# A small language-model tower in float32: block orders in the expert part and the latent stage, a small Silu at a turn's end, and identity products in TensorE's waits

## The reference, cut to what matters

```python
h = _L0_tok_ref(x, ...)                      # embedding, positions, layer norm
h = h + _L0_attn_ref(_layernorm(h), ...)     # attention, 12 heads, fake-quantised
h = h + _L0_ffn_ref(_layernorm(h), ...)      # feed-forward of layer 0: 3 causal attention experts, gated
h = h + _L1_attn_ref(_layernorm(h), ...)     # latent stage: linear attention, then silu(xn @ w1) * (xn @ w2) @ w3
h = h + _L1_ffn_ref(_layernorm(h), ...)      # attention, router, 8 experts

# in _L0_ffn_ref, with x normalised
qk = x @ Wqk + bqk ; ve = x @ Wv[e] + bv[e] ; gate = softmax(relu(x @ Wg1 + bg1) @ Wg2 + bg2)
# in _L1_attn_ref, 192 -> 512 -> 192
latent = silu(x_norm @ w_comp)
ffn_out = silu(xn @ w1) * (xn @ w2) @ w3
# in _L1_ffn_ref, each token in its two best experts, 192 -> 768 -> 192
h = gelu(xm @ w1[e] + b1[e], approximate=False)
out = out + combine[:, e:e + 1] * (h @ w2[e] + b2[e])
```

## Time and profile before

| what | value |
|---|---|
| median of three runs | 2048.46 us |
| the profiled execution | 2050.18 us |
| its span, first to last instruction | 2048.5 us |
| TensorE (PE) busy | 1606.7 us, 78% |
| VectorE (DVE) busy | 1309.3 us, 64% |
| ScalarE (ACT) busy | 976.1 us, 48% |
| GpSimd (POOL) busy | 400.1 us, 20% |
| mean granted TensorE clock | 0.862 |

### The profile page before, as it was taken

The page is one execution under the profiler, slowest core; times in us unless marked ns, Lnnn a source line. Parts: engine busy times, 40 slices in busy tenths (PEclk is TensorE's granted clock), DMA queues, the critical chain, the costliest instruction groups (busy, mean ns, idle before and its releaser), DMA issues.

```text
span 2048.5 us, 36437 instructions
## 1 busy us (share of the span) xinstructions
PE 1606.7 (78%) x12540; PEld 1167.9 (57%) x12540; DVE 1309.3 (64%) x4361; ACT 976.1 (48%) x2773; POOL 400.1 (20%) x494
## 2 busy tenths in 40 slices
PE   0166673978888668888888868999999769999996
PEld 0032222865665445555555547777877647777774
DVE  7898885878888777887787844666666622222121
ACT  1275998944444444455555423344444324444441
POOL 7302332000000100000000010222222223333332
PEclk9985555557788779999999978999999979999998
DMA  3000001049960000000000000000000057777775
GB/s 73 16 1 1 1 1 17 6 95 185 181 97 0 1 1 1 0 0 0 0 0 0 0 26 1 25 24 23 23 23 27 20 138 178 179 181 175 185 175 128
DMA packets 136262, 113.00 MB, mean 55 GB/s; under 512 B 29416, under 2 KB 128456, under 8 KB 136136
## 3 DMA queue, kind: packets, MB, share of 16 engines
q1 hardware_dynamic: 119320, 91.70, 19.4%
q0 software_dynamic: 16864, 20.33, 5.2%
HBM read 69.19 MB, written 45.94 MB: 56 GB/s over the span
## 4 chain that ended last, share of the span: by engine, by line
PE 51%; DVE 27%; ACT 15%; issue 4%; POOL 1%; DMA 0%; DVEq 0%; ACTq 0%; POOLq 0%; SPq 0%
ACT bank L716 8%; PE bank L2331 8%; PE bank L1007 6%; PE bank L2316 5%; PE bank L2320 4%; PE bank L1987 3%; PE bank L1000 2%; PE bank L1217 2%; PE bank L1665 2%; PE bank L966 2%; DVE R L1839 2%; DVE WK L1581 1%; DVE R L1581 1%; PE bank L2015 1%; PE bank L2000 1%
## 5 line engine op out<-in xcount | busy, mean ns | idle before, releaser
L1047 POOL TENSOR_TENSOR WK<-WK,mhalf 128x2 f32<-128x2 f32 (+1 forms) x96 | 78.0, 813 | 837.4 <-DVE WK L1505 328.3
L2368 ACT ACTIVATE R<-bank,R 128x256 f32<-128x256 f32 x234 | 98.3, 472 | 217.9 <-PE bank L2320 217.9
L2220 DVE SCALAR_TENSOR_TENSOR WK<-bank,R,WK 128x192 f32<-128x192 f32 x78 | 28.9, 412 | 266.6 <-PE bank L2331 266.6
L716 ACT ACTIVATE bank<-bank,nbias,sc 128x128 f32<-128x128 f32 x384 | 168.9, 952 | 21.7 <-POOL nbias L528 21.7
L1007 PE MATMUL bank<-WK,R 96*128 96x256 f32 x576 | 159.1, 421 | 17.0 <-ACT WK L973 11.0
L2249 POOL DMA_INDIRECT moe_sum<-WK x78 | 121.6, 1558 | 258.4 <-DVE WK L2220 197.2
L2331 PE MATMUL bank<-R 128*128 128x192 f32 x936 | 169.1, 331 | 0.0
L716 ACT ACTIVATION_READ_ACCUMULATOR bank<-bank,nbias,sc 128x1 f32 x384 | 162.2, 727 | 0.0
L2331 PEld LDWEIGHTS bank<-R 128*128 128x128 f32 x936 | 150.1, 190 | 13.3 <-issue 13.3
L1007 PEld LDWEIGHTS bank<-WK,R 96*128 96x128 f32 x576 | 111.3, 204 | 41.6 <-ACT WK L973 15.6
L2316 PE MATMUL bank<-R 128*128 128x256 f32 x468 | 126.1, 392 | 1.1 <-ACT R L2359 1.1
(11 more groups left out here) (496 smaller groups left out, 3971.2 us busy)
## 6 DMA issues: line engine op xcount, KB each, us to landing
moe_rows_in<-zeros SPq DMA_DIRECT2D x1, 25026.0 KB, 146.2
R<-in_L_ffn_w SPq DMA_DIRECT2D x39, 576.0 KB, 5.0
R<-in_L_ffn_w SPq DMA_DIRECT2D x39, 384.0 KB, 3.0
R<-moe_rows_in SPq DMA_DIRECT2D x39, 194.0 KB, 4.7
R<-in_L_ffn_w SPq DMA_DIRECT2D x78, 96.0 KB, 3.7
R<-in_L_ffn_b SPq DMA_DIRECT2D x39, 96.0 KB, 5.4
moe_sum<-resid POOLq DMA_DIRECT2D x16, 192.0 KB
moe_sum<-WK POOLq DMA_INDIRECT x78, 5.9
```

The source lines that it names most:

```text
L716: ins = nc.scalar.activation(s, s, ACT.Exp, bias=nbias[:, u, k:k + 1], scale=col(SS), accum_out=units(sum_all, g, u)[:, k:k + 1])
L2368: ins = nc.scalar.activation(x_hid[q], bank[(0, 2, 0)[p] + n][:, 0:NR], ACT.Gelu, bias=xb_1[h][:, q:q + 1])
```

## The change

1. **Expert part.** All six half-height products of a group come first, into six banks (0 to 5), then the six full ones onto them, then the transposes of the next group, then all twelve down products, into the two halves of one bank (7). `up` no longer waits for gelus within a group. ScalarE takes the next group's rows behind the third pair of gelus instead of the second.
2. **Latent stage.** `hidden` runs four full and four half-height products for `p = 0`, and four half-height and four full ones for `p = 1`.
3. **Latent stage, ScalarE.** A Silu of one column (`scalar_l_silu`) is the `over` of the stage.
4. **Feed-forward of layer 0.** Products of the identity with itself, into bank 3, which is then overwritten: five ahead of the wait for the normalised rows, two between the transposes and the wait for their copy.

```diff
+        def stirred_f(a, n):
+            for _ in range(n):
+                nc.tensor.matmul(a.bank[3][:, 0:P], ident[:, :], ident[:, :], start=True, stop=True)
         def tensor_f_1(pe, g, a, f):
+            stirred_f(a, 5)
             pe.wait_ge(f.x, per(g, 1, 1))
             turn(a, a.x, 0, f.xTp)
+            stirred_f(a, 2)
             pe.wait_ge(f.xT, per(g, 1, 1))
             product(a, fw_qk, slice(0, P), a.bank[3][:, 0:NM]).then_inc(f.qk_p, 1)
...
             in_turns_apart(act, lambda g, a: scalar_l_1(act, g, a, l_signals(a)),
-                           lambda g, a: scalar_l_2(act, g, a, l_signals(a)))
+                           lambda g, a: scalar_l_2(act, g, a, l_signals(a)), lambda: scalar_l_silu())
...
         def hidden(a, f, p):
-            for wa, wb, out in ((lw_1a, lw_1b, slice(0, NM)), (lw_2a, lw_2b, slice(NM, 2 * NM))):
-                for n in range(2):
-                    c = 2 * p + n
-                    nc.tensor.matmul(a.bank[c][:, out], wa[:, c * P:(c + 1) * P], a.xT[:, 0, :], start=True, stop=False)
-                for n in range(2):
-                    s = slice(HE * n, HE * (n + 1))
-                    mm = nc.tensor.matmul(a.bank[2 * p + n][:, out], wb[s, p * P:(p + 1) * P], a.xT[s, 1, :], start=False,
-                                          stop=True)
-            mm.then_inc(f.hid_p, 1)
+            first, second = slice(0, NM), slice(NM, 2 * NM)
+            def wholes():
+                for w, out in ((lw_1a, first), (lw_2a, second)):
+                    for c in (2 * p, 2 * p + 1):
+                        mm = nc.tensor.matmul(a.bank[c][:, out], w[:, c * P:(c + 1) * P], a.xT[:, 0, :], start=(p == 0 and w is lw_1a),
+                                              stop=(p == 1), skip_group_check=True)
+                return mm
+            def rests():
+                for w, out in ((lw_1b, first), (lw_2b, second)):
+                    for n in range(2):
+                        s = slice(HE * n, HE * (n + 1))
+                        mm = nc.tensor.matmul(a.bank[2 * p + n][:, out], w[s, p * P:(p + 1) * P], a.xT[s, 1, :],
+                                              start=(p == 1 and w is lw_1b), stop=(p == 0), skip_group_check=True)
+                return mm
+            if p == 0:
+                wholes()
+                rests().then_inc(f.hid_p, 1)
+            else:
+                rests()
+                wholes().then_inc(f.hid_p, 1)
...
+        def scalar_l_silu():
+            nc.scalar.activation(still[:, 1:2], mhalf[:, 0:1], ACT.Silu)
...
-                    ins = nc.vector.scalar_tensor_tensor(out=x_y[h][:, t, :], in0=bank[4 + t][:, 0:D], scalar=w(t),
+                    ins = nc.vector.scalar_tensor_tensor(out=x_y[h][:, t, :], in0=bank[7][:, t * D:(t + 1) * D], scalar=w(t),
...
+        def hidden_at(p, n):
+            return bank[2 * p + n][:, 0:NR]
...
-            def up(g, h, p, first=False):
-                if p == 0:
-                    pe.wait_ge(x_xT, per(g, B3, h + 1))
-                    pe.wait_ge(x_w[h], per(g, 96, 96))
-                    if h > 0 or not first:
-                        pe.wait_ge(x_gelu, per(g, B3 * PAIRS, h * PAIRS))
-                elif p == 2:
-                    pe.wait_ge(x_gelu, per(g, B3 * PAIRS, h * PAIRS + 1))
-                b = (0, 2, 0)[p]
+            def up_rests(g, h, first=False):
+                pe.wait_ge(x_xT, per(g, B3, h + 1))
+                pe.wait_ge(x_w[h], per(g, 96, 96))
+                if h > 0 or not first:
+                    pe.wait_ge(x_gelu, per(g, B3 * PAIRS, h * PAIRS))
+                for p in range(PAIRS):
+                    for n in range(2):
+                        s = slice(HE * n, HE * (n + 1))
+                        nc.tensor.matmul(hidden_at(p, n), xw_1b[h][s, p * P:(p + 1) * P], x_T[h][s, 1, :], start=True, stop=False)
+
+            def up(h, p):
                 for n in range(2):
                     q = p + PAIRS * n
-                    nc.tensor.matmul(bank[b + n][:, 0:NR], xw_1a[h][:, q * P:(q + 1) * P], x_T[h][:, 0, :], start=True,
-                                     stop=False)
-                for n in range(2):
-                    s = slice(HE * n, HE * (n + 1))
-                    mm = nc.tensor.matmul(bank[b + n][:, 0:NR], xw_1b[h][s, p * P:(p + 1) * P], x_T[h][s, 1, :], start=False,
-                                          stop=True)
+                    mm = nc.tensor.matmul(hidden_at(p, n), xw_1a[h][:, q * P:(q + 1) * P], x_T[h][:, 0, :], start=False, stop=True)
                 mm.then_inc(x_up, 1)
...
-                        mm = nc.tensor.matmul(bank[4 + t][:, 0:D], x_hid[f][:, t * P:(t + 1) * P], xw_2[h][:, f, :],
-                                              start=(p == 0 and n == 0), stop=(p == PAIRS - 1 and n == 1))
+                        mm = nc.tensor.matmul(bank[7][:, t * D:(t + 1) * D], x_hid[f][:, t * P:(t + 1) * P], xw_2[h][:, f, :],
+                                              start=(p == 0 and n == 0 and t == 0), stop=(p == PAIRS - 1 and n == 1),
+                                              skip_group_check=True)
...
             def group_of(g, h, more, first=False):
-                up(g, h, 0, first)
-                up(g, h, 1)
+                up_rests(g, h, first)
+                for p in range(PAIRS):
+                    up(h, p)
                 if more:
                     turn_rows(*((g, h + 1) if h < B3 - 1 else (g + 1, 0)))
-                down(g, h, 0)
-                up(g, h, 2)
-                down(g, h, 1)
-                down(g, h, 2)
+                for p in range(PAIRS):
+                    down(g, h, p)
...
-                    if p == 1 and more:
-                        take_rows(*((g, h + 1) if h < B3 - 1 else (g + 1, 0)))
+                if more:
+                    take_rows(*((g, h + 1) if h < B3 - 1 else (g + 1, 0)))
```

More of the change, by code:

```diff
@@ L2367, in group_of @@
                         q = p + PAIRS * n
-                        ins = nc.scalar.activation(x_hid[q], bank[(0, 2, 0)[p] + n][:, 0:NR], ACT.Gelu,
-                                                   bias=xb_1[h][:, q:q + 1])
+                        ins = nc.scalar.activation(x_hid[q], hidden_at(p, n), ACT.Gelu, bias=xb_1[h][:, q:q + 1])
                     ins.then_inc(x_gelu, 1)
-                    if p == 1 and more:
-                        take_rows(*((g, h + 1) if h < B3 - 1 else (g + 1, 0)))
+                if more:
+                    take_rows(*((g, h + 1) if h < B3 - 1 else (g + 1, 0)))
             take_rows(0, 0)
```

## The result

The changed kernel takes **1988.4 us** (median of four runs, 1983.8 to 1992.7) against 2048.5 in the same comparison: ratio 0.9705, 95% interval 0.9682 to 0.9728, 60 us faster. The sign and most of the mechanisms came out as written; the sum was short by 15 us, because GpSimd's stores did not fall behind, the blocks of the feed-forward gained more than they were given, and a stage without an edit gained too.

What follows compares the result with a forecast made beforehand. TensorE was taken to bound the expert part, with its clock at 0.80 in the feed-forward. Gains of 25 (expert), 2 and 4.5 (latent) and 14 (feed-forward) sum to 45.5 us: 2003 us against the median 2048.46, range 1989 to 2022.

Steps and rivals of the forecast that it cites:

- (a) to (c): Expert part: taking of next rows covered by 2.2 us, output bank emptied 3 us early, rows arriving with 2 us to spare.
- (d): Expert part: GpSimd's adding stores need 9.1 us a round and fall behind; 8.7 to 8.8 us taken on average.
- the 5 us: Expert part: the lag of GpSimd's stores left at the end, about 5 us.
- Rival 1: Expert part: GpSimd's stores set the pace, rounds of 9.36 us, gain 7 instead of 25, 2021 us; chance 0.13.
- rival 2: Feed-forward: the identity products do not hold the clock, +16 instead of -14 us, 2033 us; chance 0.08.
- I put its bound at 14.7 us: Feed-forward: VectorE's bound of a block, 14.7 us where it ends a turn, 14.1 otherwise.
- Less 16 x 0.15 for delays: Feed-forward: the identity products delay each of 16 blocks by 0.15 us, taken off the gain.
- The slope of 0.38: Feed-forward: 0.38 us gained for each microsecond at the low clock (79 us), giving the upper bound of 30 us.
- Rival 4: Latent stage: the loop's table loads lie on the way in full, 18 us instead of 4.5, 1990 us; chance 0.05.
- Rival 3: Latent stage: it cools, with half-turns at a lowered clock, 22 us more, 2025 us; chance 0.06.

Runs made afterwards that it cites:

- expert order: The kernel before with only the new order of the expert part's blocks, output bank included: 2018.7 us, ratio 0.9853.
- four changes: The kernel before with four changes of height in a group of the expert part where it had six: 2034.7 us, ratio 0.9939.
- one bank: The kernel before with a group's down products in the two halves of bank 7, in the order of before: ratio 0.9998.

## Why the prediction fell short

- **Expert part, 25 forecast, 29.8 measured.** TensorE's arithmetic was right (8.61 forecast, 8.63 measured, 0.2 us a change of height), covers (a) to (c) held. The step that failed is (d), "A round is then 1.86 + 6.4 + about 0.8 = 9.1 us". The 0.8 was read in rounds that VectorE's output released. A store that is held by its predecessor's landing alone starts under 0.3 us behind it, in about half of the rounds (the store from 1799.50 lands after 6.1 us: 1.86 + 6.1 + 0.3 make the 8.2 of that round). With second landings of 5.1 to 7.3 us, mean 6.3 without the last three groups, such a round is 1.86 + 6.3 + 0.27 = 8.4 us on average, under TensorE's 8.62. No store is late at the end, so the 5 us that were subtracted for that were not there. Rival 1 fell with it.
- **Feed-forward, 14 forecast, 21.7 measured.** The mechanism was right (the clock rose to 1.00 throughout, rival 2 did not come true). Three sizes were off. "I put its bound at 14.7 us (14.1 without the turn's end)": it is 14.28 and 13.89, so five long blocks gave 10.7 instead of 8.3, three 5.6 instead of 4.3, one 1.1 instead of 0.8, and five short ones 2.4 instead of 1.0. "Less 16 x 0.15 for delays": there are none, and even seven products more cost 0.45 us a block on average, where they add 1.5 us of work. The first block gave 1.2 and the last one 0.8, 2.0 together against the 1.5 forecast. The bound was VectorE's busy time with a guessed share of idle steps in its chain. No block of before had its clock at 1.00; the short ones, 14.35 at 0.88, came nearest, and I allowed them 0.2 us more where it was 0.45. The slope of 0.38 in the upper bound does not come out of the earlier trace rows either: 1.48 us over 3.4 to 3.6 us more at the low level is 0.41 to 0.43. It bears on the bound alone.
- **Latent stage, 6.5 forecast, 6.1 measured.** At a clock of 1.00 the small Silu gives 0.93 us a turn and the order of the products 0.28; the forecast was 0.93 less 0.2 for the small Silu, and 0.30. The first block gains nothing, as forecast, since the load put before the loop takes the place of the one at the loop's first latent Silu (34.70 us against 33.43 + 1.30; the first two windows are of before):

```profile
720.44:753.87 33.43, 18.09 (x138) 13.02 (x138) 20.61 (x66) 11.91 (x29) 1.70 (x2) 0.62 0.00 1
753.87:755.17 1.30, 1.13 (x4) 0.68 (x4) 1.12 (x3) 1.29 (x2) 0.00 (x0) 1.00 0.00 0
698.15:732.85 34.70, 18.88 (x142) 13.53 (x142) 21.75 (x68) 11.99 (x30) 1.70 (x2) 0.64 0.00 1
```

Six times 0.93 and seven times 0.28 are 7.5 us. Half-turns at a lowered clock add 4.5 us where those of before added 3.4, and one at 1.00 is 0.3 longer than its like. So the sum came near its forecast partly by luck: what the small Silu did not cost and what the clocks took nearly cancel. Rival 4 (both loads in full) is excluded. Rival 3 came true for three half-turns of 14 (31.64, 29.54 and 29.11 us) where before it was two. Its "thirteen of fifteen stay at 1.00" was misread: the first block was at 0.62 already, so it was twelve.
- **Joint, 0 forecast, 4.0 measured.** Its instructions are untouched; its clock differs. With no edit ahead of it (before, expert order, four changes, one bank) it took 103.7 us all four times; with any edit ahead of it, 97 to 101. The step that failed is a term put at nothing: the sum treats stages without edits as constants. Such dips also go with the spread of the executions of one kernel: 9 us for the changed one (mean granted clock 0.882 in the fastest, 0.877 in the slowest), 10 for the small Silu alone (0.868 and 0.861). What decides where they fall was not tested and stays open.

The sum of the four parts alone is 30.1 + 24.8 + 7.2 + 7.0 = 69 us, by ratio, against 60 for the whole. The latent parts alone are worth 7.5 by their turns, and 14.2 by these ratios: the stretches behind an edit gained in each single run (2.3, 9.6 and 6.0 us in the profiled ones), and in the whole only once (4.1).

## What to carry to other kernels

When the rows show TensorE's clock fall in a stage that has idle waits, price the stage by blocks at either clock and find out first which engine bounds a block with the clock up; a few products without effect, in waits that are idle anyway, can then be worth as much as a reordering, and here two gave 19 us where seven gave 22. Group products by the height of the array that they use. When an edit shifts the start of later stages, keep a few us of range for clocks there, on both sides.

## What the runs showed of the hardware

- Two products a block of 14 us, 0.4 us of extra work, were enough to lift the mean granted clock of 452 to 660 us from 0.79 to 0.92; five lifted it to 0.97.
- The clock does not rise with busy time alone: in the first layer's attention TensorE is busy throughout at 0.50, its lower level, with products of which most read 32 rows (L640, L641). No run here tried other products there.

```profile
360.00:420.00 60.00, 60.00 (x1033) 53.78 (x1030) 51.91 (x164) 56.11 (x117) 0.00 (x0) 0.50 0.02 4
```

- A change between full and half height costs 0.18 to 0.21 us on average over the expert part; the single pieces of the earlier trace rows show 0.15 in front of transposes and 0.20 elsewhere.
- 24 instructions in a row into one bank (3.90 us in the changed kernel) take as long each as 8 that alternate between two (1.30 us before).
